# GpSimd's group-wide jobs cut into pairs of tiles, the heads' channels laid out in halves again, and the second pass written in another order

## Time and profile before

| | |
|---|---|
| median of 3 runs | 1629.18 us (1626.99 to 1632.07) |
| profiled execution, its own time | 1630.66 us |
| its span in the trace | 1628.8 us |
| PE busy | 1601.6 us, 98% |
| DVE / ACT / POOL busy | 1275.5 / 978.0 / 786.7 us |

### The profile page before, as it was taken

One profiled execution on the slowest core, in us unless ns is written; L12 is line 12 of the kernel. 1 busy time (PEld: TensorE's weight loads), 2 busy tenths in 40 slices (PEclk: granted clock), 3 DMA queues, 4 the chain that ended last, 5 costly groups with the idle time before them and its releaser, 6 DMA issues.

```text
span 1628.8 us, 30435 instructions
## 1 busy us (share of the span) xinstructions
PE 1601.6 (98%) x10977; PEld 1443.2 (89%) x10977; DVE 1275.5 (78%) x2487; ACT 978.0 (60%) x1770; POOL 786.7 (48%) x752
## 2 busy tenths in 40 slices
PE   8999999999999999999999999999999999999998
PEld 6878888888789998989999999989899999999997
DVE  6686655546688797978888887979788888889787
ACT  6665665656465747475565657474756666564744
POOL 4564553434232636355544546363544444463637
PEclk9999999999999999999999999999999999999999
DMA  7332322232411111121121112111111221111110
GB/s 228 114 95 73 130 65 94 97 121 78 157 47 55 53 54 53 55 108 56 65 91 47 60 55 107 55 53 55 52 55 62 94 101 64 54 54 55 53 54 27
DMA packets 85922, 123.96 MB, mean 76 GB/s; under 512 B 9983, under 2 KB 58251, under 8 KB 84750
## 3 DMA queue, kind: packets, MB, share of 16 engines
q1 hardware_dynamic: 85774, 122.02, 22.5%
HBM read 86.86 MB, written 35.14 MB: 75 GB/s over the span
## 4 chain that ended last, share of the span: by engine, by line
PE 82%; DVE 10%; issue 3%; ACT 3%; POOL 2%; DMA 1%; SPq 0%; DVEq 0%; POOLq 0%; ACTq 0%
PE QH L81 11%; PE QH L82 11%; PE QH L83 11%; PE AC L81 7%; PE AC L83 7%; PE AC L82 7%; PE GU L81 5%; PE GU L83 5%; PE GU L82 5%; PE TT L832 2%; PE DN L724 2%; PE DN L81 2%; PE DN L82 2%; PE DN L83 2%; DVE rl L1849 1%
## 5 line engine op out<-in xcount | busy, mean ns | idle before, releaser
L2328 POOL TENSOR_TENSOR hb<-hb,rs_h 128x704 f32<-128x704 f32 x64 | 89.0, 1391 | 206.5 <-DVE rs_h L1687 206.5
L1251 ACT ACTIVATE hb<-GU 128x352 f32<-128x352 f32 x128 | 59.3, 463 | 214.8 <-PE GU L83 214.8
L1204 ACT ACTIVATE rh<-QH 128x512 fp32r<-128x512 f32 x256 | 150.3, 599 | 39.4 <-DVE QH L1840 36.1
L81 PE MATMUL GU<-wgh,xqh 128*128 128x352 f32 x512 | 169.6, 331 | 2.9 <-DVE hb L1680 2.9
L83 PE MATMUL GU<-wgh,xql 128*128 128x352 f32 x512 | 165.1, 322 | 0.0
L82 PE MATMUL GU<-wgl,xqh 128*128 128x352 f32 x512 | 164.9, 322 | 0.0
L2334 POOL TENSOR_TENSOR hb<-hb,sn_h 128x64 f32<-128x64 f32 x64 | 18.8, 293 | 299.0 <-DVE hb L1692 299.0
L1855 DVE TENSOR_TENSOR rl<-QH,rh 128x512 fp32r<-128x512 f32 x128 | 85.9, 682 | 83.9 <-ACT rh L1204 81.7
L81 PE MATMUL AC<-w2h,rh 128*128 128x256 f32 x512 | 146.1, 285 | 0.0
L81 PE MATMUL AC<-Mh,rh 128*128 128x256 f32 x512 | 145.1, 283 | 0.1
L82 PE MATMUL AC<-w2l,rh 128*128 128x256 f32 x512 | 142.7, 279 | 0.0
(11 more groups left out here) (237 smaller groups left out, 5594.1 us busy)
## 6 DMA issues: line engine op xcount, KB each, us to landing
zb<-z_scratch SPq DMA_DIRECT2D x128, 256.0 KB, 3.4
xa<-in_L_attn_src SPq DMA_DIRECT2D x16, 512.0 KB, 4.1
xt_scratch<-xth SPq DMA_DIRECT2D x32, 256.0 KB, 2.9
xt_scratch<-xtl SPq DMA_DIRECT2D x32, 256.0 KB, 3.0
xb<-in_L_attn_src SPq DMA_DIRECT2D x16, 512.0 KB, 4.2
xnTh<-xt_scratch SPq DMA_DIRECT2D x16, 512.0 KB, 5.0
xnTl<-xt_scratch SPq DMA_DIRECT2D x16, 512.0 KB, 6.2
out<-x SPq DMA_DIRECT2D x15, 512.0 KB, 7.0
```

The lines of the kernel that those rows point to most:

```text
L81: e.matmul(outp, lh, rh, start=start, stop=False, skip_group_check=check)
L1204: e.activation(RH[j % 4][:], src, ACT.Copy).then_inc(S[sem], 1)
L1251: e.activation(HB[i % 3][:, hf * HALF:(hf + 1) * HALF], gu_bank(i, hf)[:, 0:HALF], ACT.Tanh, scale=0.5).then_inc(S["th"], 1)
L2328: e.tensor_tensor(hb, hb, spread(rs_h[i % 2][:], 44), ALU.mult).then_inc(S["hin"], 1)
```

## The change

Three things.

1. GpSimd's five group-wide jobs take a pair of tiles as argument (512 columns an instruction), and their semaphores count pairs: `final_add(g, 0)` and `final_add(g, 1)` for `final_add(g)`, and so on.
2. The orders of the second pass are others on PE, ACT, DVE and GpSimd, by some places.
3. The heads' channels lie in halves again: partitions 0 to 63 are one head, 64 to 127 the other. Wq, G and KV are copied straight, K's sums are copied by four instructions on 64 partitions each for four masked ones on 128, the parity column is gone, and `z_in` reads each of its two rows 64 times in a row.

```diff
 def z_in(g, j):
     w.wait_ge(S["zo"], 16 * (g + 1))
     w.wait_ge(S["zq"], 8 * g + j - 3)
-    e.dma_start(ZB[j % 4][:], z_dram[g, 2 * j:2 * j + 2].unsqueeze(0).broadcast_to([64, 2, 512])).then_inc(S[f"zb{j % 4}"], 16)
+    e.dma_start(ZB[j % 4][:], z_dram[g, 2 * j:2 * j + 2].unsqueeze(1).broadcast_to([2, 64, 512])).then_inc(S[f"zb{j % 4}"], 16)
...
-    for head in range(2):
-        for c0 in (head, 16 + head):
-            e.tensor_scalar(ksA[:, c0:c0 + 239:34], ksum[:], parity[:, head:head + 1], None, ALU.mult).then_inc(S["A_ks"], 1)
+    for p in (0, 64):
+        for c0 in (p // 64, 16 + p // 64):
+            e.tensor_copy(ksA[p:p + 64, c0:c0 + 239:34], ksum[p:p + 64, :]).then_inc(S["A_ks"], 1)
...
-    e.tensor_copy(kvt[p:p + 64, 4 * hf:4 * hf + 4, p // 64:128:2],
+    e.tensor_copy(kvt[p:p + 64, 4 * hf:4 * hf + 4, p:p + 64],
...
-def x2_affine(g):
-    x = x1[g % 2]
-    w.wait_ge(S["lnbn"], 4 * g + 4)
-    w.wait_ge(S["half"], 2)
-    e.tensor_tensor(x[:], x[:], rows4("g2"), ALU.mult).then_inc(S["lnbs"], 1)
-    w.wait_ge(S["lnbs"], 2 * g + 1)
-    e.tensor_tensor(x[:], x[:], rows4("be2"), ALU.add).then_inc(S["lnbs"], 1)
+def x2_affine(g, pr):
+    x = x1[g % 2][:, 2 * pr:2 * pr + 2, :]
+    w.wait_ge(S["lnbn"], 4 * g + 2 * pr + 2)
+    w.wait_ge(S["half"], 2)
+    e.tensor_tensor(x, x, rows2("g2"), ALU.mult).then_inc(S["lnbs"], 1)
+    w.wait_ge(S["lnbs"], 4 * g + 2 * pr + 1)
+    e.tensor_tensor(x, x, rows2("be2"), ALU.add).then_inc(S["lnbs"], 1)
...
-def final_add(g):
-    w.wait_ge(S["us"], g + 1)
-    e.tensor_tensor(x1[g % 2][:], x1[g % 2][:], Xb[g % 2][:], ALU.add).then_inc(S["fo"], 1)
+def final_add(g, pr):
+    x = x1[g % 2][:, 2 * pr:2 * pr + 2, :]
+    w.wait_ge(S["us"], 2 * g + pr + 1)
+    e.tensor_tensor(x, x, Xb[g % 2][:, 2 * pr:2 * pr + 2, :], ALU.add).then_inc(S["fo"], 1)
...
 # VectorE, in the loop over groups
     z_mul(g, 6)
     z_mul(g, 7)
     gate_mul(b, 1)
     z_lo(g, 6)
     z_lo(g, 7)
     h_round(a)
-    g_mul(c - 4)
     gate_mul(c, 1)
```

More of the change, by code:

```diff
@@ L647, in kv_map @@
                             o = (j % 4) * 128 + p
-                            paired_ch = slice(j * 128 + p // 64, j * 128 + 128, 2)
-                            last = e.matmul(bank[p:p + 64, o:o + 64], wv_s[:, kt, ch], gt[:, kt, paired_ch if kt else ch], start=kt == 0, stop=kt == 1,
+                            last = e.matmul(bank[p:p + 64, o:o + 64], wv_s[:, kt, ch], gt[:, kt, ch], start=kt == 0, stop=kt == 1,
                                             skip_group_check=True, tile_position=(0, p))
@@ L907, in _ @@
             m_map(NB - 1, 1)
+            turn_xq(0, 0)
             q_proj(0, 4)
             q_proj(0, 5)
+            gate_up(0, 1)
             m_map(NB - 1, 2)
@@ L913, in _ @@
             q_proj(0, 7)
-            gate_up(0, 1)
+            gate_up(0, 0)
             den_sums(0)
-            gate_up(0, 0)
+            turn_xq(0, 1)
             gate_up(1, 0)
-            turn_xq(0, 1)
             gate_up(1, 1)
@@ L944, in _ @@
             f_step(0, 2)
+            turn_h(1, 0)
             h_proj(0, 6)
-            turn_h(1, 0)
-            f_step(0, 3)
             turn_h(1, 1)
             h_proj(0, 7)
+            f_step(0, 3)
             q_proj(1, 0)
             down(1)
+            turn_h(2, 0)
             q_proj(1, 1)
-            turn_h(2, 0)
             gate_up(3, 1)
@@ L987, in _ @@
                 gate_up(c, 0)
-                turn_h(a, 0)
                 down(d - 4)
                 turn_x1(g, 0)
+                turn_h(a, 0)
                 turn_x1(g, 1)
@@ L1097, in split_w @@
                 else:
-                    rows = paired(src_w[:, m0, :]) if n == 1 else src_w[:, m0:m1, :]
-                    o = hi[:, m0, :].rearrange("p (j q s) -> p j q s", s=2, q=64) if n == 1 else hi[:, m0:m1, :]
-                    e.activation(o, rows, ACT.Copy).then_inc(S["A_wsh"], 1)
+                    e.activation(hi[:, m0:m1, :], src_w[:, m0:m1, :], ACT.Copy).then_inc(S["A_wsh"], 1)
             def ln_apply(i):
@@ L1458, in _ @@
                 z_hi(g, 5)
-                z_hi(g, 6)
-                z_hi(g, 7)
+                g_tanh(c - 4)
                 h_abs(a)
-                gate_tanh(c, 1)
                 ln_norm("lnb", g - 1, 0)
@@ L1465, in _ @@
                 ln_norm("lnb", g - 1, 2)
+                z_hi(g, 6)
+                z_hi(g, 7)
                 ln_norm("lnb", g - 1, 3)
+                gate_tanh(c, 1)
                 gate_tanh(c, 0)
@@ L1470, in _ @@
                 x1_hi(g, 0)
-                g_tanh(d - 4)
                 h_hi(a, 0)
                 x1_hi(g, 1)
+                g_tanh(d - 4)
                 h_hi(a, 1)
@@ L1477, in _ @@
                 gelu(g, 1)
+                h_abs(b)
+                g_tanh(a)
                 gelu_hi(g, 1)
[L1479 to L1485, removed]
+            gate_tanh(NT - 1, 0)
+            gelu(NG - 1, 2)
+            gelu_hi(NG - 1, 2)
+            gelu(NG - 1, 3)
+            gelu_hi(NG - 1, 3)
+            gelu(NG - 1, 4)
+            h_abs(NT - 2)
             h_hi(NT - 3, 0)
             h_hi(NT - 3, 1)
-            h_abs(NT - 2)
-            gelu(NG - 1, 4)
             gelu(NG - 1, 5)
+            gelu_hi(NG - 1, 4)
             gate_tanh(NT - 1, 1)
+            gelu_hi(NG - 1, 5)
             g_tanh(NT - 3)
-            gelu_hi(NG - 1, 4)
-            gelu_hi(NG - 1, 5)
+            gelu(NG - 1, 6)
             h_hi(NT - 2, 0)
+            gelu_hi(NG - 1, 6)
+            gelu(NG - 1, 7)
+            gelu_hi(NG - 1, 7)
             h_hi(NT - 2, 1)
             h_abs(NT - 1)
[L1498 to L1501, removed]
+            g_tanh(NT - 2)
             h_hi(NT - 1, 0)
-            g_tanh(NT - 2)
             h_hi(NT - 1, 1)
@@ L2070, in _ @@
             gelu_lo(0, 1)
+            gelu_lo(0, 2)
             h_round(1)
-            gelu_lo(0, 2)
-            gate_mul(3, 0)
             gelu_lo(0, 3)
@@ L2076, in _ @@
             gelu_lo(0, 5)
+            h_lo(1, 0)
+            g_mul(0)
+            h_round(2)
+            gelu_lo(0, 6)
+            h_lo(1, 1)
+            gelu_lo(0, 7)
             x_max(1, 0)
-            h_lo(1, 0)
             x_scale(1, 0)
[L2080 to L2084, removed]
+            gate_mul(3, 0)
+            q_elu(1, 0)
+            h_lo(2, 0)
             x_round(1, 0)
-            h_lo(2, 0)
-            q_elu(1, 0)
             q_elu(1, 1)
+            h_lo(2, 1)
             gate_mul(3, 1)
-            h_lo(2, 1)
-            x_max(1, 1)
             h_max(3)
@@ L2189, in _ @@
                 q_elu(g + 1, 7)
+            gate_mul(NT - 4, 0)
             x_round(NG - 1, 1)
-            gate_mul(NT - 4, 0)
             den_inverse(NG - 1)
@@ L2414, in x1_residual @@
+            def x1_residual(g, pr):
+                x = x1[g % 2][:, 2 * pr:2 * pr + 2, :]
+                if pr:
+                    w.wait_ge(S["lnad"], 2 * g + 2)
+                else:
+                    w.wait_ge(S["lnan"], 2 * g + 2)
+                w.wait_ge(S["x1T"], 2 * g + pr + 1)
+                e.tensor_tensor(x, x, rows2("g1"), ALU.mult).then_inc(S["xab"], 1)
                 w.wait_ge(S["vb2"], 1)
-                w.wait_ge(S["xab"], 2 * g + 1)
-                e.tensor_tensor(x[:], x[:], rows4("b2"), ALU.add).then_inc(S["xab"], 1)
@@ L2555, in _ @@
             ln1_rstd(NG - 1, 1)
-            x2_affine(NG - 2)
-            final_mul(NG - 2)
+            x2_affine(NG - 2, 1)
             h_in(NT - 3)
-            final_add(NG - 2)
+            final_mul(NG - 2, 0)
+            final_mul(NG - 2, 1)
+            h_in(NT - 2)
+            final_add(NG - 2, 0)
             h_out(NT - 3)
-            h_in(NT - 2)
+            h_out(NT - 2)
+            x1_residual(NG - 1, 0)
+            x1_residual(NG - 1, 1)
             last_shift(0)
-            h_out(NT - 2)
+            last_scale(0)
             h_in(NT - 1)
-            last_scale(0)
+            h_out(NT - 1)
             last_shift(1)
-            h_out(NT - 1)
             last_scale(1)
-            last_residual(0)
-            last_residual(1)
             last_shift(2)
-            last_scale(2)
+            final_add(NG - 2, 1)
             last_rstd(0)
             last_rstd(1)
+            last_scale(2)
             last_shift(3)
```

260 lines of the change are left out of this document (124 added, 136 removed).

## The result

The changed kernel takes 2184.8 us (median of 4, 2184.6 to 2186.3) against 1629.0 for the kernel before: a ratio of 1.342, 95% interval 1.340 to 1.343. The forecast was 2185. It was right in its mechanism; its size came out so closely because two errors cancelled, as the experiments show.

What follows compares the result with a forecast made beforehand. PE was taken as the bound, busy 1601.6 of 1628.8 us. The profiled 1630.7 plus z_in's 557 (34.8 a group, 16 groups), pairs, orders and the rest at 0, made 2188, 2186 against the median, given as 2185; range 2100 to 2295.

Steps and rivals of the forecast that it cites:

- That two engines carry each load: z_in's zb loads, second pass: an outermost source dimension of 2 puts every load on two engines, the same two each time.
- 5.4 us a load: Each z_in load of zb on two engines: 5.4 us, 43.2 for a group's eight, bounds 5.3 and 6.2.
- The chain behind the last load: After a group's eighth load: z_mul 0.65, gate_mul 1.03, gate_up(c, 1) 1.92, hand-overs 0.3; at_step 6 starts 32.5 us later.
- The clock: PE behind a group's last wait: a granted clock lowered in the waits costs 2.3 us a group, bounds 0 and 3.4.
- The orders at 0: New second-pass orders on four engines: 0; gain bounded by PE's 6 us of idle time, loss allowed 15 us.
- The pattern's sum: z_in's new pattern: 32.5 + 2.3 = 34.8 us a group, 557 us for 16 groups.
- The four buffers: zb's four buffers don't slow the loads: z_mul j-4 frees one while three more loads wait in the queue.
- Rival A: z_in: the pattern does not matter, the issue splits by the 128 partitions; 1623 to 1632 us; chance 5%.
- B: z_in's two engines don't pipeline across loads: 7.6 us each, 246 us in all, 2430 us; chance 6%.
- C: z_in's packets as slow as the crowded ones: 6.2 us a load adds 102 us, 2290 us; chance 12%.
- D: PE's clock holds at 1.00, or emptier queues take back part of the stall: 2115 us; chance 17%.
- The signs: Profile after: landing 15 to 20 us, DMA share 0.13 at 48 GB/s, period 109 us, PE near 70%, clock 0.50.

Runs made afterwards that it cites:

- e1: The changed kernel with z_in's source read as 64 repetitions of both rows again: 1650.8 us, 1.013 to the kernel before.
- e4: The changed kernel with z_in reading four rows 32 times each, outermost dimension 4, the same 256 KB: 1830.8 us, 1.124 to the kernel before.
- e12: The changed kernel with z_in's loads cut to half their bytes from the second group on, outermost dimension still 2: 1858.4 us, 1.141 to the kernel before.
- e9: The changed kernel with 24 zero-adding matmuls on PE at three waits of each group from the second on: 2159.6 us, 1.326 to the kernel before.
- e10: The kernel before with the pairs and all four new orders, channels' layout and z_in as before: 1651.1 us (1.014).
- e5: The kernel before with GpSimd's five jobs cut into pairs, all orders else as before: 1628.4 us (1.0005).
- e11: The kernel before with the pairs and all four new orders, but gelu_hi(g, 1) ahead of g_tanh(a) on ScalarE: 1635.8 us (1.004).

## Why the prediction was right, point by point

- **That two engines carry each load**: right. It was read from the one transfer with a short outermost dimension (z_out, four engines), and e1 to e4 and e12 show it: 2 gives a share of 0.13, 4 gives 0.27, and one line costs 538 us in the kernel before and 534 in the changed one. The prediction's price for four engines, some 350 us less, is what e4 gave: 354.
- **5.4 us a load**: 5.29 measured, so eight take 0.9 us less than in the sum, 14 us over 16 groups. The row of the other transfers with every engine busy (5.3) was nearer than the crowded stretch of the loads themselves (6.2).
- **The chain behind the last load** (gate_mul, gate_up, at_step 6): right. Forecast 32.5 us and 2.3 for the clock, 34.8; measured 33.3 to at_step 6 and 1.3 behind it, 34.6. The 33.3 hold 3.65 - 1.92 = 1.7 us of slow gate_up; without it they are 31.6, 0.9 under the sum's. The 1.3 behind it are 0.5 of the clock (3.26 - 2.75) and some 0.8 of the new orders, of which 0.47 is the wait at 1274.12. So even the group's 34.6 hold a part that the sum had at nothing.
- **The clock**: granted 0.50 when the last wait ends, as forecast from a stretch of the first pass. It costs 1.7 us in gate_up and 0.5 in at_step 6 and 7 in this group, 2.2 where 2.3 stood in the sum; e9 got back 25.2 us, 1.8 for each of the 14 groups that have the zero matmuls.
- **The orders at 0**: the term that was mis-sized. "With PE waiting 30 us in each group most of it is covered" failed: the one wait of the new orders that could be traced lies at h_proj(g, 3), 18.9 us behind at_step 6, where PE has no stall left that would cover it; it is 8.4 us in e10 and 7.5 in the changed kernel. In all, the orders cost 21.7 us by themselves, and the changed kernel takes 2184.8 - 2167.3 = 17.5 more than the pattern alone, both more than the loss of 15 that I allowed.
- **The pattern's sum**, 557 us, measured alone: 538. 14 of the 19 us too many come from the 5.4. They and the 17.5 that were left out cancelled. The total's 0.2 us of error is luck; its parts were each off by some 20.
- **Pairs at 0**: right (e5). **Layout at 0**: right (e10 and e1 within 0.3 us).
- **The four buffers**: they cost nothing, as the sum had it, but not for its reason. Three more loads don't wait in the queue: SP is held at each issue (see the last section). The DMA share stays at 0.13 all the same, so the two engines never ran dry.
- **Rival A** (pattern without effect) and **B** (7.6 us a load, the next one's data waiting for the landing of the last) fell, the latter by the 5.29; **C** (6.2 us a load) too. D's held clock is what e9 made by force; it is worth 25 us.
- **The signs**: a share of 0.13 at 51 GB/s (48 forecast), a period of 109.1 us, z_mul's wait as DVE's longest and a clock of 0.50 in each group came. PE busy near 70% did not: it is 80%, since PE's busy time itself rose from 1601.6 to 1753.6 us, matmuls at the half clock taking longer. The profile gives no time to landing for these loads; the eighth load of group 7 is issued at 1230.38 and its z_mul starts at 1249.71, 19.3 us later, within the 15 to 20 forecast.

Open: the 6.2 us that e11 keeps over the kernel before (1.004, 1.003 to 1.006), and what the orders cost outside the wait at h_proj(g, 3). No run parts them.

## What to carry to other kernels

Read the access pattern of a transfer from its outermost dimension, on both sides: a broadcast written as [2, 64, n] and one as [64, 2, n] move the same bytes, and the first runs on two engines. Before such a line is changed, look in the trace for a transfer with a short outermost dimension and compare its DMA share with 1/16 per engine. Where the layout asks for halves, two transfers of 64 rows each cost 6 us here over the old pattern, one of [2, 64] 528 more than those two. And price an order by the first call that would wait behind another engine's late signal (here g_tanh ahead of gelu_hi); a big stall elsewhere in the loop did not cover it here. Try orders that were written for each other together: two parts of them cost 134 and 201 us here, where the whole costs 21.7.

## What was not expected of the hardware

- The issue itself blocks. An SP issue of a zb load took 559 ns (median) before; on two engines with all bytes it takes 5147 ns, about one load's time, and with four engines or half the bytes it is short again (502 and 476 ns). The tile's rows in the changed kernel, then in e4 and in e12:

```profile
L404 SPq DMA_DIRECT2D zb<-z_scratch x128: 495/5147/6547, 439.6 to 2105.3; - x128
```

```profile
L404 SPq DMA_DIRECT2D zb<-z_scratch x128: 499/502/910, 440.8 to 1757.0; - x128
```

```profile
L405 SPq DMA_DIRECT2D zb<-z_scratch x128: 474/476/5582, 439.2 to 1789.2; - x128
```

  The waiting for a free buffer is not in these durations: the third and the fourth issue of group 7, for which the z_muls of the group before had freed the buffers, take 2.74 and 5.73 us already.

```profile
1206.21 2.74 SPq L404 DMA_DIRECT2D zb<-z_scratch  x1
1209.00 5.73 SPq L404 DMA_DIRECT2D zb<-z_scratch  x1
```

  The z_muls wait for the data in any case, and the two engines stayed busy, so no cost of it is seen here. What stands behind on SP (the next group's loads, the store) can't be issued meanwhile; no run shows a price for that.
- Work added in a wait made the kernel 25.2 us faster, with gate_up(c, 1) at a granted clock of 1.00 in place of 0.50; twice as much of it made it 168 us slower.
